# VectorE's copy of the gathered high rows moved into the next step, and the statistics of the incoming x moved behind conv 1's eviction, in a two-layer depthwise convolution

## The reference, cut to what matters

```python
def _gn(v, G=32, eps=1e-5):              # group norm, 12 channels a group
    g = v.reshape(B_, G, C_ // G, H_, W_)
    m = jnp.mean(g, axis=(2, 3, 4), keepdims=True)
    s = jnp.var(g, axis=(2, 3, 4), keepdims=True)
    return ((g - m) / jnp.sqrt(s + eps)).reshape(v.shape)
...
# x: (8, 384, 128, 128) float32
x = x + _L0_conv_ref(_gn(x), L0_conv_k)       # depthwise 3x3, padding 1
x = x + _L1_conv_ref(_gn(x), L1_conv_weight)  # depthwise 7x7, padding 3, weight averaged over 4 rotations
return x
```

## Time and profile before

| | |
|---|---|
| median of 3 runs | 3432.22 us |
| the profiled execution's own time | 3437.14 us |
| its span in the trace | 3435.3 us |
| mean granted TensorE clock | 0.953 |
| busy: PE, DVE, ACT, POOL | 85%, 80%, 63%, 47% |

### The profile page before, as it was taken

One profiled execution on the slowest core, in us unless ns is written; L12 is line 12 of the kernel. 1 busy time (PEld: TensorE's weight loads), 2 busy tenths in 40 slices (PEclk: granted clock), 3 DMA queues, 4 the chain that ended last, 5 costly groups with the idle time before them and its releaser, 6 DMA issues.

```text
span 3435.3 us, 76363 instructions
## 1 busy us (share of the span) xinstructions
PE 2912.2 (85%) x28676; PEld 1839.2 (54%) x28676; DVE 2756.5 (80%) x5180; ACT 2176.9 (63%) x3969; POOL 1613.0 (47%) x1553
## 2 busy tenths in 40 slices
PE   0468888989898889888888889898989989898995
PEld 0245555555555555555555555555555555555553
DVE  3548888888788888888878888888888888788885
ACT  1346666666676667666666666666666766676672
POOL 3324544544455445454444445444445544454552
PEclk9888999999999999999999999999999999999998
DMA  2698888888888888888888888888878888888866
GB/s 88 174 222 216 210 212 215 218 208 213 219 214 222 213 215 210 209 211 211 224 214 205 209 215 217 216 217 214 215 208 218 215 215 215 211 210 219 214 171 156
DMA packets 955769, 712.41 MB, mean 207 GB/s; under 512 B 92166, under 2 KB 893958, under 8 KB 955334
## 3 DMA queue, kind: packets, MB, share of 16 engines
q1 hardware_dynamic: 549894, 506.13, 58.8%
q10 hardware_dynamic: 405504, 201.38, 20.9%
HBM read 259.73 MB, written 220.81 MB: 140 GB/s over the span
## 4 chain that ended last, share of the span: by engine, by line
SPq 46%; DVE 26%; DMA 11%; issue 8%; POOL 5%; PE 2%; ACT 1%; ACTq 0%; DVEq 0%; POOLq 0%
SPq L235 15%; DMA BT<-H 10%; SPq L256 9%; SPq L245 9%; SPq L247 8%; DVE BT L508 5%; POOL H L635 5%; DVE H L475 4%; DVE X L502 4%; SPq L275 4%; DVE BN L484 4%; DVE X L453 2%; SPq L296 1%; PE PS L743 1%; PE PS L714 1%
## 5 line engine op out<-in xcount | busy, mean ns | idle before, releaser
L714 PE MATMUL PS<-H,BAND 128*128 128x512 f16 x6912 | 1617.4, 394 | 108.6 <-DMA BAND<-rows 72.3
L643 POOL TENSOR_TENSOR H<-Z,H 128x512 f16<-128x512 f32 x768 | 864.5, 1128 | 1422.0 <-ACT Z L554 1421.6
L743 PE MATMUL PS<-BT,BAND 118*32 118x512 f16 x21504 | 1273.4, 395 | 172.7 <-DVE X L453 140.6
L714 PEld LDWEIGHTS PS<-H,BAND 128*128 128x128 f16 x6912 | 1026.7, 152 | 654.1 <-issue 127.7
L743 PEld LDWEIGHTS PS<-BT,BAND 118*32 118x32 f16 x21504 | 792.1, 132 | 643.2 <-issue 307.9
L551 ACT ACTIVATE H<-X,RB 128x512 f16<-128x512 f32 x768 | 618.8, 806 | 493.4 <-DVE H L475 482.0
L635 POOL TENSOR_SCALAR H<-X,RB 128x512 f16<-128x512 f32 x768 | 721.9, 954 | 353.0 <-DVE RB L442 344.5
L508 DVE COPY BT<-BT 39x8512 f16<-39x8512 f16 x192 | 464.4, 2419 | 457.2 <-DMA BT<-H 455.1
L534 ACT ACTIVATE Z<-X,RB 128x512 f32<-128x512 f32 x768 | 562.2, 804 | 109.0 <-DVE RB L442 83.6
L554 ACT ACTIVATE Z<-X,RB 128x512 f32<-128x512 f32 x768 | 615.7, 802 | 0.0
L577 ACT ACTIVATE DUMP<-X 128x512 bf16<-128x512 f32 x768 | 476.5, 622 | 139.4 <-DVE X L502 139.4
(11 more groups left out here) (47 smaller groups left out, 418.7 us busy)
## 6 DMA issues: line engine op xcount, KB each, us to landing
X<-in_x SPq DMA_DIRECT2D x768, 256.0 KB, 4.1
out_y<-X ACTq DMA_DIRECT2D x768, 256.0 KB, 5.3
BT<-H SPq DMA_DIRECT2D x384, 162.1 KB
BT<-H SPq DMA_DIRECT2D x384, 149.6 KB
BT<-H SPq DMA_DIRECT2D x576, 99.8 KB
BT<-H SPq DMA_DIRECT2D x384, 62.3 KB
BT<-H SPq DMA_DIRECT2D x192, 83.1 KB
rows<-v_all SPq DMA_DIRECT2D x8, 1638.0 KB, 10.9
```

Source lines behind the costliest of these rows:

```text
L643: g.tensor_tensor(part(H1, n, 1, img, O1, P1), Z[:, img, :].rearrange("p (c w) -> p c w", c=CC), part(H1, n, 0, img, O1, P1), ALU.subtract ...
L714: last = mm(PA[:, ch, :], band[:, j, ws, :], data[:, :, O1 - 1 + j:O1 - 1 + j + W], start=k == 0, stop=k == 3 * K1 - 1)
L743: last = mm(banks2(n)[b * BL:(b + 1) * BL, ch, :], band[:, j, :], rows, start=j == 0, stop=j == K2 - 1, tile_position=(0, b * BL))
```

## The change

VectorE's order within a slot is changed; every other engine's program is untouched, and so is the count of instructions. The copy of chunk n moves from the end of slot n+3 to slot n+4, between the subtractions and the eviction of conv 1. The statistics of chunk t+4 move behind that eviction.

```diff
-                n = t + 4
+                n = t - 4
                 if real(n):
-                    c = n % CPU_
-                    dve.wait_ge(x_loaded[n % BODY], (at(n - n % BODY) // BODY + 1) * (16 * NI))
-                    for img in range(NI):
-                        v.bn_stats(BN[:, c, img, :], xs(n, img)).then_inc(bn_done, 1)
-                    if c == CPU_ - 1:
...
+                    dve.wait_ge(high_gathered[n % 2], ((at(n) - n % 2) // 2 + 1) * HIGH_LANDED)
+                    v.tensor_copy(BT[AGAIN:AGAIN + WIN, n % 2, :, :, :].rearrange("p b c l -> p (b c l)"),
+                                  BT[0:WIN, n % 2, :, :, :].rearrange("p b c l -> p (b c l)")).then_inc(high_again, 1)
                 n = t
                 if real(n):
                     c = n % CPU_
...
-                n = t - 3
+
+                n = t + 4
                 if real(n):
-                    dve.wait_ge(high_gathered[n % 2], ((at(n) - n % 2) // 2 + 1) * HIGH_LANDED)
-                    v.tensor_copy(BT[AGAIN:AGAIN + WIN, n % 2, :, :, :].rearrange("p b c l -> p (b c l)"),
-                                  BT[0:WIN, n % 2, :, :, :].rearrange("p b c l -> p (b c l)")).then_inc(high_again, 1)
+                    c = n % CPU_
+                    dve.wait_ge(x_loaded[n % BODY], (at(n - n % BODY) // BODY + 1) * (16 * NI))
+                    for img in range(NI):
+                        v.bn_stats(BN[:, c, img, :], xs(n, img)).then_inc(bn_done, 1)
+                    if c == CPU_ - 1:
...
```

More of the change, by code:

```diff
@@ L477, in slot @@
                                         part(H2, n, 0, img, O2, P2), ALU.subtract).then_inc(lo_done[1], 1)
+                n = t - 4
+                if real(n):
+                    dve.wait_ge(high_gathered[n % 2], ((at(n) - n % 2) // 2 + 1) * HIGH_LANDED)
+                    v.tensor_copy(BT[AGAIN:AGAIN + WIN, n % 2, :, :, :].rearrange("p b c l -> p (b c l)"),
+                                  BT[0:WIN, n % 2, :, :, :].rearrange("p b c l -> p (b c l)")).then_inc(high_again, 1)
+                n = t
+                if real(n):
+                    c = n % CPU_
+                    g = at(n - n % GCH) // GCH
+                    dve.wait_ge(conv1_done, at(n) + 1)
+                    for img in range(NI):
+                        v.scalar_tensor_tensor(xs(n, img), PA[:, :, img * W:(img + 1) * W],
+                                               SC[:, 0, bass.ds(g, 1)], xs(n, img), ALU.mult, ALU.add,
+                                               accum_out=SS[:, c, img, 0:1]).then_inc(y_done, 1)
                 n = t + 4
@@ L494, in slot @@
                         v.tensor_tensor(MQ1[:, :, 1], MQ1[:, :, 1], TMP[:, 0, 0], ALU.add).then_inc(mq_ready, 1)
-                n = t
-                if real(n):
-                    c = n % CPU_
-                    g = at(n - n % GCH) // GCH
-                    dve.wait_ge(conv1_done, at(n) + 1)
-                    for img in range(NI):
-                        v.scalar_tensor_tensor(xs(n, img), PA[:, :, img * W:(img + 1) * W],
-                                               SC[:, 0, bass.ds(g, 1)], xs(n, img), ALU.mult, ALU.add,
-                                               accum_out=SS[:, c, img, 0:1]).then_inc(y_done, 1)
-                n = t - 3
-                if real(n):
-                    dve.wait_ge(high_gathered[n % 2], ((at(n) - n % 2) // 2 + 1) * HIGH_LANDED)
-                    v.tensor_copy(BT[AGAIN:AGAIN + WIN, n % 2, :, :, :].rearrange("p b c l -> p (b c l)"),
-                                  BT[0:WIN, n % 2, :, :, :].rearrange("p b c l -> p (b c l)")).then_inc(high_again, 1)
                 if t > NCH:
```

## The result

The changed kernel takes 3513.55 us, the median of 4 runs (3498.03 to 3518.16), against 3429.25 us before (4 runs on the same chip): a ratio of 1.023, 95% interval 1.0204 to 1.0255. The forecast was 3552 us, slower, with a range of 3340 to 3615. The profiled execution is the fastest of the four, 3498.03 us with a span of 3496.2; it stands 15.5 us under the median.

A forecast was written before the change was run, and what follows sets the result against it. TensorE's two convolutions and VectorE's chain between them were taken to bound the loop, the late gather entering through the copy. Slots of 19.3, 15.05 and 18.35 us, mean 17.57 against 16.88, add 120 us: 3552 us, range 3340 to 3615.

The forecast's parts named there:

- The wait for the gather goes: VectorE ahead of its copy: asked for one slot later, the copy no longer waits for the gather, 2.2 us a slot.
- TensorE waits for the copy instead: Ahead of conv 2: TensorE stands for the copy in two slots of three, 2.95 us and 2.5 us.
- The copy loses the port: Behind the subtractions: GpSimd's piece starts 0.14 us ahead and shuts the copy out; its mean goes from 2.41 to 3.1 or 3.2 us.
- Rival 1: At the port shared with GpSimd: the copy comes first and takes 2.38 us; 3310 to 3355 us, chance 0.18.
- rival 2: At the port shared with GpSimd: the copy loses only in kind 0 slots; 3447 us, chance 0.12.
- rival 4: Gather still late, or GpSimd's delayed low parts hold conv 1: + 50 us or more; chance 0.05, shared with others.
- The price of the second edit: Statistics and aggregation behind conv 1's eviction delay L686 by 0.5 us in one slot of three.
- The clock: Conv 2 after TensorE's wait: the granted clock falls and conv 2 takes 8.00 us instead of 6.34, costing 1.65 us.
- three in five: Conv 2 of kind 2 slots: share taken to be slow after a wait of 2.5 us, + 1.0 us.
- of the 12 waits over 2.6 us all 12: Kernel before: every such wait ahead of conv 2 was followed by a slow one, so kind 0 was counted always slow.
- Rival 3: Conv 2 after TensorE's wait: port lost as forecast, but the clock stays up at 2.95 and 2.5 us; 3397 us, chance 0.05.
- That the clock makes the loss: Slot sum: the waits alone give 16.68 us, less than the present 16.88; the clock's falls bring it to 17.57.

The follow-up runs named there:

- e5: The changed kernel with 18 extra matmuls in TensorE's wait for the copy, in two slots of three: 3364.08 us, 0.9808 of the kernel before.
- e4: The changed kernel with GpSimd's low parts of layer 1 made to wait for the copy: 3472.32 us, 1.0119 of the kernel before.
- e8: The kernel before with only the copy moved, plus 18 extra matmuls in TensorE's wait in two slots of three: 3375.8 us, ratio 0.9856.
- e9: The changed kernel with GpSimd's low parts behind the copy and 3 extra matmuls in TensorE's wait: 3309.09 us, 0.9655 of the kernel before.
- e7: The changed kernel with 9 extra matmuls in TensorE's wait for the copy, in two slots of three: 3434.37 us, 1.0019 of the kernel before.
- e3: The changed kernel with the copy ahead of the subtractions instead of behind them: 3410.95 us, 0.9938 of the kernel before.

## Why the prediction was right, and where its sizes were off

**The wait for the gather goes.** Right: from 383.5 us to none that the rows name.

**TensorE waits for the copy instead.** Right, by its steps and sizes: waits of 2.95 us in kind 0, none to speak of in kind 1 and 2.5 in kind 2 were forecast, 3.25, 0.27 and 2.71 measured. Of the missing 0.2 to 0.3 us, 0.11 are that conv 2 starts 0.26 us behind the copy's end (1572.98, 1573.24), where I took the 0.15 that it stands behind an eviction, and 0.05 a conv 1 of 8.03 instead of 8.08; the rest is spread over the steps ahead. The 0.26 are not the copy's doing: e5 shows 0.15 behind the same copy where the wait for it is the last that TensorE has, as the wait for an eviction was.

**The copy loses the port.** Right: 0.14 us of lead for GpSimd, a copy of 3.18 us. e4 shows the cause by taking it away: the copy has 2.37 us again, and the waits shrink by 0.8 us. By the Trainium skill's rule ("SBUF — State Buffer", section "Who interferes with whom") the loser stands for the other's whole instruction. The trace agrees: the copy always ended 2.23 us behind GpSimd's first piece, near the 2.37 that it takes alone, and GpSimd's second piece 0.95 behind the copy, near the 1.09 that it takes alone. Rival 1, which needed the copy to come first, is out; so is rival 2, since the copy took 3.15, 3.19 and 3.21 us in kinds 0, 1 and 2. So is rival 4: the copy's row keeps 5.5 us of idle time, and conv 1 waits for nothing.

**The price of the second edit.** 0.5 us in kind 1 was forecast for the aggregation behind the eviction. There is none: L687 follows conv 2 without a wait in all 58 slots (1562.25, where conv 2 ends at 1562.32), since L509 had ended at 1561.98. The eviction of conv 1, the statistics and the aggregation took 6.22 us (1555.76 to 1561.98) where I had counted 6.8; 0.58 of that is L507, 0.28 us instead of the 0.86 of the row that I used. Counted as the forecast did, from the end of one conv 2 to that of the next, the slots of kinds 0, 1 and 2 took 19.03, 14.62 and 17.92 us; 19.3, 15.05 and 18.35 were forecast (the table counts from conv 1 to conv 1). And e5 against e8 has the edit gain 0.03 us a slot. What I had overlooked is that, with the copy moved, eviction and statistics stand behind one another in either order, ahead of the same L686, so that the order has no price.

**The clock.** This is the term that was mis-sized. I had the conv 2 of kind 0 always slow (1.65 us a slot) and that of kind 2 in three of five (1.0 us). In the profiled execution 41 of 58 and 23 of 58 were: 7.57 and 7.00 us on the mean instead of 8.00 and 7.34, so 1.23 and 0.66 us. That is 0.25 of the 0.38 us between 17.57 and the measured 17.19; kind 1 is 0.14. The three in five was a choice between 8 of 16 and 12 of 12, and it was two in five. Part of that is chance: the other three runs took 3509 to 3518 us at mean clocks of 0.946 to 0.951, against 0.953 and 3498 in the profiled one. What failed is "of the 12 waits over 2.6 us all 12": of the 58 waits of 3.25 us in the changed kernel 17 were followed by a conv 2 at full speed, and in e4 all 58 waits of 1.88 us by a slow one. The direction stood the test, the statistics of a dozen waits did not. Nor was 8.89 the longest conv 2 of that trace: one at 1788.57 took 9.31 us. The mean clock, which was to fall from 0.953 to 0.94, is 0.953 in the profiled execution. Rival 3, a clock that stays up, is out with 64 falls.

**That the clock makes the loss**: said in the sum (16.68 us a slot without it, under the 16.88 of before). Half of this is shown. The falls cost the change 0.63 us a slot by its own trace, twice its loss of 0.31, and e5, which has hardly any, takes 16.48 us and is 1.9% faster than the kernel before. But the comparison is not even. The 16.88 us hold falls as well, while the forecast counted every conv 1 of the new order at 8.08 us and did not say that this takes away those of before (8.43 us on the mean before, 8.05 after). Measured at the same mean clock, 0.96, the change lost 53.5 us over the 174 slots, and 46 of them are TensorE's standing. What is shown is that the change swaps falls that lay in conv 1 and conv 2 for falls in conv 2 alone, in two kinds of slot, where conv 2 stands on the path. Whether the falls of before were hidden behind the late gathers, and so cost less, is open.

**How much of it was luck.** Little in the direction: the new wait and the lost port, which make it, came as forecast. The range of 3340 to 3615 was wide enough to hold a gain too, so that the time lies in it says little. The time came out 38 us under the forecast, since both mis-sized terms, the clock and the aggregation, were too dear.

What is still open: what decides, beside its length, whether a stand is followed by a fall. e9 and e4 have stands of 1.89 and 1.91 us in kinds 0 and 2 with 12 falls of 58 and 58 of 58. I did not vary the time at which a stand begins by itself, and e4, whose rounds all took the same time, leaves that as a rival.

## What to carry to other kernels

When a late transfer is waited for by an engine's program order, moving the wait a step later removes it; then write down, slot by slot, what now stands between the release of the next matmul group and its start, since that sum, and not the engine's busy share, is the new path. Count the kernel before with its own falls of the clock, or give both the same remedy, before you say what the clock costs. A wait of two to three microseconds on TensorE costs more than its length when the clock falls behind it: look at the length of the matmul group that follows, and try matmuls without use in the wait before giving up the order. An instruction of VectorE that GpSimd shuts out, as it did this copy (3.18 us instead of 2.37), should be placed where GpSimd has nothing ready, or GpSimd be made to wait for it. Matmuls and wait together (e9) turned a loss of 2.3% into a gain of 3.4%.

## What the runs showed of the hardware that was not expected

- The mean granted clock, 0.93 in e4's 174 slots against 0.96 in the change, was lowest where the waits were shorter, and there all 116 conv 2s were slow, in 58 rounds of three slots of 51.20 us each (51.14 to 51.30).
- Three extra matmuls (0.49 us) in each of 116 waits (e9) lifted the mean clock over those slots from 0.93 to 0.99.
- How soon conv 2 starts behind what it waited for goes by the order of TensorE's waits. It was 0.26 us behind the copy where a wait for `out_done`, met long before, follows the wait for the copy; 0.15 us where the wait for the copy, or for an eviction, is the last; and 0.05 us where extra matmuls stand ahead of the wait (e5, e7, e8).
- A short lead does not hold the port. In the kernel before, a GpSimd piece (L635) recorded 0.01 to 0.05 us ahead of the copy took 2.96 to 2.99 us instead of 0.77, and the copy 2.37 to 2.40; in e3 the same went for leads of 0.06 to 0.07 us (2.99 to 3.00). A piece recorded 0.09 us ahead or more kept its 0.77 us, and the copy took up to 2.90.
